# Graph attention and a routed feed-forward block on one core: seven loads move to SP's queue at batch 10, edge ends come in pairs, node features two blocks at a time

## The chip, the core and the metric

The kernel runs on one core of a Trainium2 chip. The core has a matrix engine (PE), a vector engine (DVE), an activation engine (ACT), GpSimd (POOL) and a synchronising engine (SP). Each has its own instruction stream; they meet only through semaphores. SP and ACT each issue transfers on a queue of their own (q1 and q10 in the profile), POOL issues gathers by index (q0). All transfers share 16 DMA engines. The metric is the device time of one execution in microseconds; lower is better.

## The reference

There are 12500 nodes with 256 features and 200000 edges sorted by target. A graph attention layer with 4 heads is followed by a feed-forward layer that is applied to the half of the nodes with the largest routing weight.

```python
src = jnp.concatenate([edge_index[0], loops])
dst = jnp.concatenate([edge_index[1], loops])
xp = (x @ W).reshape(n, H, C)
a_src = jnp.einsum('nhc,hc->nh', xp, att_src)
a_dst = jnp.einsum('nhc,hc->nh', xp, att_dst)
alpha = jax.nn.leaky_relu(a_src[src] + a_dst[dst], negative_slope=0.2)
ex = jnp.exp(alpha - amax[dst])
denom = jax.ops.segment_sum(ex, dst, num_segments=n)
w = ex / denom[dst]
msg = xp[src] * w[..., None]
agg = jax.ops.segment_sum(msg, dst, num_segments=n)
...
_, idx = jax.lax.top_k(weights, k)
sel = jnp.take_along_axis(x, sel_idx[:, :, None], axis=1)
h = jax.nn.gelu(jnp.einsum('bkd,dh->bkh', sel, w1) + b1)
y = jnp.einsum('bkh,hd->bkd', h, w2) + b2
...
x = x + gnn(layernorm(x), ...)
x = x + ffn(layernorm(x)[None], ...)[0]
```

## The kernel before

The nodes are cut into 98 blocks of 128. The program has three stages.

**The node stage** takes the blocks in 14 batches of 7 (`batches`). SP loads a batch of x into one of four rooms (`load_x`, L405; batch g+4 is loaded when batch g has been normalised). DVE takes statistics and normalises (`batch_stats`, `norm`, L1046), with POOL giving the reciprocal root (`rstd_batch`). PE transposes each block (L852), ACT copies the transposed block to SBUF (L710), PE multiplies it by the extended weight matrix (`project`, L829), ACT copies the product (`row_copy`, L698), and SP stores a finished batch to the table `node_rows` in HBM (`store_rows`, L417). The products have two rooms of a batch each, so ACT's first copy of batch g waits until the store of batch g-2 has landed. DVE's `keep_asd(g-2)` (L1050) waits for the last copy of batch g-2 and stands ahead of the statistics of batch g+1. In the last three batches DVE and PE also work out where each window's edges begin.

Before ACT makes its first copy it issues, one after the other on its own queue, two loads of edge targets (L677, L681) and seven loads of biases and weights (L682 to L689): b2, the attention bias, w1, w2, b1, the routing weights and the routing bias. b2 is split into parts by POOL after its last batch (`bias_parts`, L563 to L570); the other six are first waited for after the node stage.

**The window stage** has a window for each block of 128 targets (`two_by_two`, windows in pairs; b is 0 for even windows). POOL gathers 16 or 17 tiles of 128 source rows per window from `node_rows`, one indirect transfer per tile (L633), with the indices in `srci`. DVE makes one-hot matrices from the targets (L1202, L1206, L1212), looks up and forms the exponents (L1231 to L1239), and weighs the gathered rows (L1250); PE sums them by target (L948) and runs the feed-forward layer of earlier windows (L911, L926) between. In each window SP's order is: the targets of window w+1, broadcast as 16-bit numbers (`dbc`, L450), the same targets by partition (`dsti`, L434 and L436), then a wait until the gathers of window w-1 have landed, then the sources of window w+1 (`srci`, again L434 and L436), the features of block w (`base`, L487), and the block's own rows (`selfr`, L491). The two lines L434 and L436 are those of the helper `load_flat`; a transfer over 16 tiles and one over the last.

**The end** selects the half of the nodes by a search over the routing weights and adds their feed-forward rows.

Of the kernel before, what the change touches and what calls it, by code (L numbers as in the profile page):

```python
# [42 lines left out]
def build(nc, x, src, dst, W, att_src, att_dst, gbias, wr, br, w1, b1, w2, b2, out, N, E):  # L43
# [45 lines left out]
    with ExitStack() as ctx:  # L89
# [43 lines left out]
        srci = sb("srci", [P, 2, TILES], I32)  # L133
        dsti = sb("dsti", [P, 2, TILES], I32)
# [24 lines left out]
        xsrc = sb("xsrc", [P, 1], I32)  # L159
        xdst = sb("xdst", [P, 1], I32)  # L160
# [127 lines left out]
        def sems(names):  # L288
# [13 lines left out]
        ld_src, ld_dst, ld_dbc, ld_self, ld_x, gath, gath_last = (  # L302
            sem2(n) for n in ("ld_src", "ld_dst", "ld_dbc", "ld_self", "ld_x", "gath", "gath_last"))
# [11 lines left out]
        (x_src, x_dst, x_dbc, x_row, x_oht, x_step, x_oh, x_lk, x_dm, x_diff, x_ex, x_sc,  # L315
         x_go, x_done) = sems(
            "x_src x_dst x_dbc x_row x_oht x_step x_oh x_lk x_dm x_diff x_ex x_sc x_go x_done")

        m_src, m_dst, m_go, m_row, m_step, m_mask, m_tr, m_max, m_done = sems(
            "m_src m_dst m_go m_row m_step m_mask m_tr m_max m_done")  # L320
# [82 lines left out]
        def _(sp):  # L403
# [14 lines left out]

            def batch_io(g, t, b, r, q):
# [11 lines left out]
            def load_flat(into, edges, first, w, b, loaded):  # L431

                before = tiles_of(w) - 1
                sp.dma_start(into[:, b, 0:before], edges[bass.ds(first, before * P)].rearrange("(p t) -> p t", t=before)).then_inc(loaded, 16)  # L434
                with nc.allow_non_contiguous_dma("an edge to a partition"):
                    sp.dma_start(into[:, b, before:before + 1], edges[bass.ds(first + before * P, P)].rearrange("(p t) -> p t", t=1)).then_inc(loaded, 16)  # L436

# [4 lines left out]
            def load_sources(w, b, first):  # L442
                load_flat(srci, src, first, w, b, ld_src[b])

            def load_targets(w, b, first):
                if known(w, 2):

                    wait_apart(sp, (loc_ok, w - 1), (lk_ok, w - 1))
                flat = tiles_of(w) * P
                sp.dma_start(dbc[:, b, 0:flat], dst16_dram[bass.ds(first, flat)].rearrange("(a e) -> a e", a=1).broadcast_to([P, flat])).then_inc(ld_dbc[b], 16)  # L450
                load_flat(dsti, dst, first, w, b, ld_dst[b])

            load_sources(0, 0, first_edge(0))
# [15 lines left out]
            def exact_loads(w, j, k):  # L469
# [3 lines left out]
                with nc.allow_non_contiguous_dma("an edge to a partition"):  # L473
                    sp.dma_start(xsrc[:, :], src[bass.ds(first, P)].rearrange("(p t) -> p t", t=1)).then_inc(m_src, 16)
                    sp.dma_start(xdst[:, :], dst[bass.ds(first, P)].rearrange("(p t) -> p t", t=1)).then_inc(m_dst, 16)
# [19 lines left out]
            def extra_loads(w):  # L495
# [3 lines left out]
                def load(j, k):  # L499
# [4 lines left out]
                    with nc.allow_non_contiguous_dma("an edge to a partition"):  # L504
                        sp.dma_start(xsrc[:, :], src[bass.ds(at, P)].rearrange("(p t) -> p t", t=1)).then_inc(x_src, 16)
                        sp.dma_start(xdst[:, :], dst[bass.ds(at, P)].rearrange("(p t) -> p t", t=1)).then_inc(x_dst, 16)
# [37 lines left out]
        def _(pool):  # L544
# [60 lines left out]
            def gather_row(k, arrived, started):  # L605
# [4 lines left out]
                with pool.If(k < 1):  # L610
                    pool.sem_inc(started, 1)
                pool.indirect_dma_start(out=xrow[:, :], out_offset=None, in_=table,
                                        in_offset=bass.IndirectOffsetOnAxis(ap=xsrc[:, 0:1], axis=0)).then_inc(arrived, 16)

            def exact_gather(w, j, k):
                wait_apart(pool, (m_src, 16 * k + 16))
# [11 lines left out]
            def window(w, i, b):  # L628
                if not known(w, 2):
                    pool.wait_ge(ld_src[b], 32 * (i + 1))  # L630

                def gather(t, arrived):
                    pool.indirect_dma_start(out=rows[:, b, t, :], out_offset=None, in_=table,  # L633
                                            in_offset=bass.IndirectOffsetOnAxis(ap=srci[:, b, t:t + 1], axis=0)).then_inc(arrived, 16)

                last = tiles_of(w) - 1
                for t in range(last):
                    if known(w, 2) and t == 0:
                        wait_apart(pool, (ld_src[b], 32 * (i + 1)))
# [21 lines left out]
                def extra_gather(j, k):  # L661
                    wait_apart(pool, (x_src, 16 * k + 16))
# [8 lines left out]
        def _(act):  # L671
# [14 lines left out]
            with nc.allow_non_contiguous_dma("a bias by column of the hidden layer"):  # L686
                act.dma_start(b1s[:, :], b1.rearrange("(c p) -> p c", p=P)).then_inc(w_ld, 16)
            act.dma_start(wrs[:, :], bc(wr.rearrange("d o -> (d o)"), D)).then_inc(w_ld, 16)
# [774 lines left out]
```

## Time and profile before

| | |
|---|---|
| median of 3 runs | 2313.58 us (2313.06 to 2314.57) |
| the profiled execution | 2314.01 us, span of its trace 2312.2 us |
| busy: PE, DVE, POOL, ACT | 1896.5, 1609.1, 1594.0, 642.5 us |
| gathers (L633) | 1613, 1553.5 us busy |
| first gather begins, last gather begins | 149.19, 2193.30 us |
| mean granted PE clock | 0.894 of full speed |
| data moved | 365.43 MB in 244353 packets |

The span goes from the first to the last instruction of the trace. The node stage takes the first 149 us, the window stage goes on to about 2240 us, and the rest is selection and output. An engine's busy time leaves out the time in which it issues transfers, waits on semaphores or branches.

### The profile page before, as it was taken

The page shows a single profiled execution, that of the slowest core. Times are in us where ns is not written, and L with a number is a line of the kernel's source. Part 1 is how long each engine was busy: PE and PEld are TensorE (multiplying, and loading weights), DVE is VectorE, ACT ScalarE, POOL GpSimd, SP SyncE. Part 2 cuts the span into 40 slices and gives each one's busy share as a digit, 9 for nine tenths or more (in the row PEclk, how much of TensorE's full clock was granted, in tenths as well). Part 3 has the DMA queues.
Part 4 walks back from the last instruction along what each step waited for, and adds up shares of the span by engine and source line. Part 5 has one row for each costly group of instructions (what it writes and reads, how often), then busy time and mean ns, then how long its engine had stood idle before and what let it go on. Part 6 is the DMA issues. An engine that isn't in the chain of part 4 may idle for free.

```text
span 2312.2 us, 35972 instructions
## 1 busy us (share of the span) xinstructions
PE 1896.5 (82%) x9193; PEld 1610.2 (70%) x9194; DVE 1609.1 (70%) x3952; ACT 642.5 (28%) x1378; POOL 1594.0 (69%) x1675
## 2 busy tenths in 40 slices
PE   5955788888888888889888888888978888889871
PEld 4844677777777777777777777777767777777761
DVE  5756766766776667767767676777766677767748
ACT  3520222322332223322332233222322233222330
POOL 2257777777777777777777777777777777777700
PEclk9977899889899999989899999999989999999885
DMA  7645555555555555555555555555555555555448
GB/s 243 215 139 150 149 145 152 154 154 142 154 158 152 145 152 154 158 142 149 158 152 152 144 154 158 152 146 150 154 157 144 148 158 154 153 147 150 134 155 295
DMA packets 244353, 365.43 MB, mean 158 GB/s; under 512 B 90405, under 2 KB 179649, under 8 KB 244322
## 3 DMA queue, kind: packets, MB, share of 16 engines
q0 software_dynamic: 77488, 214.85, 35.0%
q1 hardware_dynamic: 150578, 134.33, 18.4%
q10 hardware_dynamic: 16256, 15.90, 2.0%
q8 instruction: 12, 0.20, 0.0%
q14 instruction: 19, 0.16, 0.0%
HBM read 326.04 MB, written 38.89 MB: 158 GB/s over the span
## 4 chain that ended last, share of the span: by engine, by line
POOL 34%; PE 25%; issue 23%; DVE 6%; POOLq 5%; DMA 4%; ACT 1%; ACTq 1%; DVEq 0%; SPq 0%
POOL rows L633 34%; PE ag_ps L948 13%; PE y_ps L926 4%; DMA rows<-node_rows,srci 3%; PE ag_ps L829 3%; POOLq L375 3%; PE h_ps L911 3%; DVE base L1438 2%; POOLq L652 1%; DVE rows L1250 1%; PE lk_ps L888 1%; PE tr_ps L852 0%; PE xl_ps L852 0%; DVE diff L1239 0%; ACT xl_ps L759 0%
## 5 line engine op out<-in xcount | busy, mean ns | idle before, releaser
L633 POOL DMA_INDIRECT rows<-node_rows,srci x1613 | 1553.5, 963 | 503.8 <-issue 474.5
L948 PE MATMUL ag_ps<-rows,oh 128*128 128x260 f32 x3322 | 921.6, 445 | 298.7 <-DVE rows L1250 297.8
L948 PEld LDWEIGHTS ag_ps<-rows,oh 128*128 128x128 f32 x3322 | 734.3, 225 | 456.0 <-issue 305.6
L1250 DVE TENSOR_TENSOR rows<-rows,xl_ps 128x768 f32<-128x768 f32 (+2 forms) x685 | 495.7, 793 | 36.4 <-ACT xl_ps L759 36.4
L926 PE MATMUL y_ps<-w2s,hT 128*128 128x256 f32 x1568 | 359.9, 383 | 6.9 <-ACT hT L740 6.9
L911 PE MATMUL h_ps<-xnT,w1s 128*128 128x256 f32 x1568 | 355.0, 379 | 0.0
L1231 DVE TENSOR_TENSOR zz<-rows,edge_dm 128x68 f32<-128x68 f32 x98 | 22.5, 229 | 470.5 <-DMA rows<-node_rows,srci 372.3
L926 PEld LDWEIGHTS y_ps<-w2s,hT 128*128 128x128 f32 x1568 | 300.7, 192 | 54.3 <-ACT hT L740 8.0
L759 ACT ACTIVATE xl_ps<-diff 128x68 f32<-128x68 f32 x98 | 22.6, 231 | 1110.2 <-DVE diff L1239 1099.7
L911 PEld LDWEIGHTS h_ps<-xnT,w1s 128*128 128x128 f32 x1568 | 297.6, 190 | 40.3
L1212 DVE TENSOR_TENSOR oh<-xl_ps,dloc 128x2176 f32<-128x2176 f32 x98 | 236.9, 2418 | 0.0
L740 ACT ACTIVATE hT<-h_ps,b1s 128x256 f32<-128x256 f32 x392 | 153.8, 475 | 1.2
L740 ACT ACT_TABLE_LOAD x98 | 125.7, 1283 | 49.4 <-ACT yb L749 34.3
L888 PE MATMUL lk_ps<-parts,dbc 128*128 (+1 forms) x1661 | 111.0, 206 | 20.0 <-DVE dbc L1202 20.0
L742 ACT ACT_TABLE_LOAD x98 | 125.7, 1283 | 1.8
L888 PEld LDWEIGHTS lk_ps<-parts,dbc 128*128 128x128 bf16 x1661 | 111.1, 160 | 20.9 <-issue 13.2
L829 PE MATMUL ag_ps<-hT,dbc 128*128 128x264 f32 x392 | 106.0, 394 | 13.4 <-ACT dbc L710 13.4
L793 ACT ACTIVATE steps_of_rows<-steps_of_rows 128x256 f32<-128x256 f32 x98 | 40.9, 417 | 199.9 <-DVE steps_of_rows L1294 199.9
L829 PEld LDWEIGHTS ag_ps<-hT,dbc 128*128 128x128 f32 x392 | 68.5, 195 | 20.9 <-issue 13.0
L1202 DVE TENSOR_SCALAR dbc<-dbc,node_id 128x2176 bf16<-128x2176 int16 x98 | 76.2, 777 | 0.0
L1219 DVE TENSOR_REDUCE edge_dm<-lk_ps 128x136 f32<-128x408 f32 x98 | 56.4, 576 | 16.1 <-issue 16.0
L588 POOL TENSOR_SCALAR rs_b<-selfr 128x7 f32<-128x7 f32 x14 | 3.9, 279 | 87.4 <-DVE selfr L1060 79.3
(183 smaller groups left out, 1322.0 us busy)
## 6 DMA issues: line engine op xcount, KB each, us to landing
dbc<-dst SPq DMA_DIRECT2D x97, 544.0 KB
rows<-node_rows,srci POOLq DMA_INDIRECT x1613, 2.7
selfr<-node_rows SPq DMA_DIRECT2D x98, 130.0 KB, 3.0
base<-in_x SPq DMA_DIRECT2D x14, 896.0 KB, 5.2
base<-in_x SPq DMA_DIRECT2D x98, 128.0 KB, 2.3
ffn_rows<-yb ACTq DMA_DIRECT2D x48, 256.0 KB, 3.3
node_rows<-base SPq DMA_DIRECT2D x13, 910.0 KB, 5.7
out<-base SPq DMA_DIRECT2D x3, 1024.0 KB, 5.8
```

The costliest lines, as they stand in the source:

```text
L375: return eng.value_load(win[0:1, bass.ds(COLS * w + k, 1)], min_val=0, max_val=most)
L633: pool.indirect_dma_start(out=rows[:, b, t, :], out_offset=None, in_=table, in_offset=bass.IndirectOffsetOnAxis(ap=srci[:, b, t:t + 1], ax ...
L740: last = nc.scalar.activation(hT[:, m, :], h_ps[:, m * PAIR:(m + 1) * PAIR], ACT.Gelu_apprx_tanh, bias=b1s[:, n:n + 1])
L742: nc.scalar.preload_act_table_set(EXP_AND_LN)
L829: last = nc.tensor.matmul(ag_ps[parity % 2][:, 0:WIDE], xnT2[:, parity % 2, c, :], wext[:, c, :], start=(c == 0), stop=(c == DC - 1))
L888: last = nc.tensor.matmul(lk_ps[:, VK * t:VK * (t + 1)], by_tile[:, t, :] if t < before else oht[:, b, before * P:(before + 1) * P], node_ ...
L911: last = nc.tensor.matmul(h_ps[:, m * PAIR:(m + 1) * PAIR], w1s[:, c, n * P:(n + 1) * P], xnT[:, c, :], start=(c == 0), stop=(c == DC - 1))
L926: last = nc.tensor.matmul(y_ps[:, a * D:(a + 1) * D], hT[:, m, a * P:(a + 1) * P], w2s[:, half * HALF + m, :], start=False, stop=(half == ...
L948: product = nc.tensor.matmul(ag_ps[b][:, 0:ROW], oh[:, b, t, :], rows[:, b, t, :], start=(t == 0), stop=False)
L1202: nc.vector.tensor_scalar(oht[:, b, 0:flat], dbc[:, b, 0:flat], node_id[:, bass.ds(w, 1)], None, ALU.is_equal).then_inc(oht_ok, 1)
L1212: nc.vector.tensor_tensor(oh[:, b, 0:n, :], iota_ps.unsqueeze(1).broadcast_to([P, n, P]), dloc[:, 0:n].unsqueeze(2).broadcast_to([P, n, P] ...
L1250: nc.vector.tensor_tensor(v, v, e, ALU.mult).then_inc(scaled[k], 1)
```

## The change

Three things are changed, and nothing of what is computed.

1. The seven loads of L682 to L689 leave ACT's stream. They are issued by SP in the same order (`load_weights`), in the turn of batch 10, right after the store of batch 9.
2. The host hands over sources and targets as one array of pairs, `edges`. `srci` and `dsti` become one tile `ends` with the two numbers side by side. Its two transfers are issued where those of the sources were, behind the wait for the gathers of window w-1. The gathers read their index from `ends[:, b, t, 0:1]`, and L1206 reads its targets from `ends[:, b, 0:n, 1]`, each with a step of 8 bytes between tiles where it was 4. For window 0 both ends are loaded at the start of the program, where only the sources were.
3. The features are loaded for two blocks at once, in the even windows.

```diff
+            def load_weights():
+
+                sp.dma_start(bias_f[0], bc(b2, D)).then_inc(b2_ld, 16)
+                sp.dma_start(gbs[:, :], bc(gbias, D)).then_inc(w_ld, 16)
+                sp.dma_start(w1s[:, :, :], w1.rearrange("(c p) n -> p c n", p=P)).then_inc(w_ld, 16)
+                sp.dma_start(w2s[:, :, :], w2.rearrange("(c p) n -> p c n", p=P)).then_inc(w_ld, 16)
...
@@ batch_io
                 if known(g, 1):
                     store_rows(g - 1, 1 - b)
+                if isinstance(g, int) and g == NB - DEEP:
+                    load_weights()
...
+            def load_ends(w, i, b, first):
+                if known(w, 2):
+
+                    wait_apart(sp, (gath[b], 16 * (TILES - 1) * i), (gath_last[b], 16 * i), (loc_ok, w - 1))
                 before = tiles_of(w) - 1
-                sp.dma_start(into[:, b, 0:before], edges[bass.ds(first, before * P)].rearrange("(p t) -> p t", t=before)).then_inc(loaded, 16)
+                sp.dma_start(ends[:, b, 0:before, :], edges[bass.ds(first, before * P), :].rearrange("(p t) v -> p t v", t=before)).then_inc(ld_ends[b], 16)
                 with nc.allow_non_contiguous_dma("an edge to a partition"):
-                    sp.dma_start(into[:, b, before:before + 1], edges[bass.ds(first + before * P, P)].rearrange("(p t) -> p t", t=1)).then_inc(loaded, 16)
+                    sp.dma_start(ends[:, b, before:before + 1, :], edges[bass.ds(first + before * P, P), :].rearrange("(p t) v -> p t v", t=1)).then_inc(ld_ends[b], 16)
...
@@ SP, window
                     load_targets(w + 1, 1 - b, first)
-                    if known(w, 1):
-
-                        wait_apart(sp, (gath[1 - b], 16 * (TILES - 1) * (i + b)), (gath_last[1 - b], 16 * (i + b)))
-                    load_sources(w + 1, 1 - b, first)
-                sp.dma_start(base[:, bass.ds(w, 1), :].rearrange("p w c -> p (w c)"), x[bass.ds(w * P, P), :]).then_inc(ld_x[b], 16)
+                    load_ends(w + 1, i + b, 1 - b, first)
+                if b == 0:
+                    sp.dma_start(base[:, bass.ds(w, 2), :], nodes(x, w, 2)).then_inc(ld_x, 16)
...
@@ POOL, window
-                                            in_offset=bass.IndirectOffsetOnAxis(ap=srci[:, b, t:t + 1], axis=0)).then_inc(arrived, 16)
+                                            in_offset=bass.IndirectOffsetOnAxis(ap=ends[:, b, t, 0:1], axis=0)).then_inc(arrived, 16)
...
@@ ACT
-            act.dma_start(bias_f[0], bc(b2, D)).then_inc(b2_ld, 16)
-            act.dma_start(gbs[:, :], bc(gbias, D)).then_inc(w_ld, 16)
-            act.dma_start(w1s[:, :, :], w1.rearrange("(c p) n -> p c n", p=P)).then_inc(w_ld, 16)
-            act.dma_start(w2s[:, :, :], w2.rearrange("(c p) n -> p c n", p=P)).then_inc(w_ld, 16)
...
@@ DVE, one_hots_turned
-                nc.vector.tensor_scalar(dloc[:, 0:n], dsti[:, b, 0:n], base_id[:, bass.ds(w, 1)], None, ALU.subtract).then_inc(loc_ok, 1)
+                nc.vector.tensor_scalar(dloc[:, 0:n], ends[:, b, 0:n, 1], base_id[:, bass.ds(w, 1)], None, ALU.subtract).then_inc(loc_ok, 1)
```

Line numbers of the changed kernel differ by a few. ACT's stream before, at its beginning: the loads of edge targets (`oh`), of b2 (`rows`), gbs, w1s, w2s, b1s, wrs and brs, and then the first copies of transposed blocks.

```order
L677 DMA oh<-in_dst 128x1600
L681 DMA oh<-in_dst 127x1
L682 DMA rows<-in_L_ffn_b 128x256
L683 DMA gbs<-in_L_gnn_bias 128x256
L684 DMA w1s<-in_L_ffn_w 128x2x1024
L685 DMA w2s<-in_L_ffn_w 128x8x256
L687 DMA b1s<-in_L_ffn_b 128x8x1
L688 DMA wrs<-in_L_ffn_wr 128x256
L689 DMA brs<-in_L_ffn_br 128x1
L710 COPY dbc<-tr_ps 128x256
L710 COPY dbc<-xl_ps 128x256
L698 COPY base<-ag_ps 128x264
```

The same place now:

```order
L682 DMA oh<-in_dst 128x1600
L686 DMA oh<-in_dst 127x1
L707 COPY dbc<-tr_ps 128x256
L707 COPY dbc<-xl_ps 128x256
L695 COPY base<-ag_ps 128x264
L707 COPY dbc<-tr_ps 128x256
```

The first copy now follows the two loads of targets directly. SP's stream before, from the last four whole stores of the node stage (batches 9 to 12) to the last piece of batch 13:

```order
L417 DMA node_rows<-base 128x7x260 x4
L450 DMA dbc<-dst 128x2176
L434 DMA dsti<-in_dst 128x16
L436 DMA dsti<-in_dst 128x1
L458 DMA window_table<-wi 98x6
L417 DMA node_rows<-base 128x5x260
L461 DMA win<-window_table 1x588
L417 DMA node_rows<-base 128x2x260
```

The same place now:

```order
L415 DMA node_rows<-base 128x7x260
L419 DMA rows<-in_L_ffn_b 128x256
L420 DMA gbs<-in_L_gnn_bias 128x256
L421 DMA w1s<-in_L_ffn_w 128x2x1024
L422 DMA w2s<-in_L_ffn_w 128x8x256
L424 DMA b1s<-in_L_ffn_b 128x8x1
L425 DMA wrs<-in_L_ffn_wr 128x256
L426 DMA brs<-in_L_ffn_br 128x1
L415 DMA node_rows<-base 128x7x260 x3
L460 DMA dbc<-dst 128x2176
L467 DMA window_table<-wi 98x6
L415 DMA node_rows<-base 128x5x260
```

The seven loads stand between the stores of batches 9 and 10, and the two small loads of targets ahead of the window table are gone. SP's stream in an odd window before (the rows without a transfer are register work and waits):

```order
L450 REGISTER_ALU
L450 DMA dbc<-dst 128x2176
L434 REGISTER_ALU
L434 DMA dsti<-in_dst 128x16
L436 ISA
L436 DMA dsti<-in_dst 128x1
L369 ISA
L434 DMA srci<-in_src 128x16
L436 DMA srci<-in_src 128x1
L487 ISA
L487 DMA base<-in_x 128x256
L491 ISA
```

The same place now:

```order
L460 REGISTER_ALU
L460 DMA dbc<-dst 128x2176
L367 ISA
L451 REGISTER_ALU
L451 DMA ends<-in_edges 128x32
L453 ISA
L453 DMA ends<-in_edges 128x2
L497 ISA
L497 DMA selfr<-node_rows 128x260
```

Both ends of the edges now stand behind the wait (the ISA row ahead of them), two transfers are gone from each window, and a third from each odd one.

## Rows read from the trace of the kernel before

**Rows 1.** The page: busy time of the engines, share of the span, instructions

```profile
PE 1896.5 (82%) x9193; PEld 1610.2 (70%) x9194; DVE 1609.1 (70%) x3952; ACT 642.5 (28%) x1378; POOL 1594.0 (69%) x1675
```

**Rows 2.** Line L633: duration ns min/median/max; idle before it until, us, times

```profile
L633 POOL DMA_INDIRECT rows<-node_rows,srci x1613: 942/947/1572, 149.2 to 2193.3; - x180
...
  issue: 474.5, 1556
  DMA node_rows<-base: 12.2, 1
  PE lk_ps L888: 9.4, 31
  PE ag_ps L948: 7.6, 25
```

**Rows 3.** Timeline of POOL, first and last gather: start, duration, [idle before]

```profile
149.19 1.12 POOL L633 DMA_INDIRECT rows<-node_rows,srci  x1 [12.22 <-DMA node_rows<-base]
...
2193.30 0.95 POOL L633 DMA_INDIRECT rows<-node_rows,srci  x1 [0.30 <-issue]
```

**Rows 4.** Timeline of ACT, 9 to 26 us (ACTq: its issuing of transfers)

```profile
9.60 0.52 ACTq L681 DMA_DIRECT2D oh<-in_dst  x1
10.15 6.13 ACTq L682 DMA_DIRECT2D rows<-in_L_ffn_b  x1
16.31 0.44 ACTq L683 DMA_DIRECT2D gbs<-in_L_gnn_bias  x1
...
17.79 3.38 ACTq L687 DMA_DIRECT2D b1s<-in_L_ffn_b  x1
21.19 3.92 ACTq L688 DMA_DIRECT2D wrs<-in_L_ffn_wr  x1
...
25.64 0.37 ACT L710 COPY dbc<-tr_ps 128x256 f32<-128x256 f32 x1 [23.28 <-issue]
```

**Rows 5.** Timeline of PE, first blocks and block 14

```profile
12.48 0.66 PE L852 MATMUL tr_ps<-ident,rows 128*128 128x128 f32 x2 [9.95 <-DVE rows L1046]
...
26.16 2.10 PE L829 MATMUL ag_ps<-hT,dbc 128*128 128x264 f32 x4 [12.59 <-ACT dbc L710]
...
44.37 0.38 PE L852 MATMUL tr_ps<-ident,rows 128*128 128x128 f32 x2
```

**Rows 6.** Timeline of DVE, batches 1 and 2

```profile
20.49 3.96 DVE L1046 TENSOR_SCALAR rows<-base,selfr,rs_b 128x256 f32<-128x256 f32 x7
38.22 0.21 DVE L1050 COPY oh<-base 128x56 f32 x1 [13.77 <-ACT base L698]
...
41.33 2.32 DVE L1046 TENSOR_SCALAR rows<-base,selfr,rs_b 128x256 f32<-128x256 f32 x7
```

**Rows 7.** Timeline of SP's queue, stores of batches 9, 10, 11 and after

```profile
109.18 0.38 SPq L417 DMA_DIRECT2D node_rows<-base  x1
118.67 0.38 SPq L417 DMA_DIRECT2D node_rows<-base  x1
129.42 0.38 SPq L417 DMA_DIRECT2D node_rows<-base  x1
...
139.38 0.88 SPq L436 DMA_DIRECT2D dsti<-in_dst  x1
140.42 0.40 SPq L458 DMA_DIRECT2D window_table<-wi  x1
...
145.69 0.24 SPq L461 DMA_DIRECT2D win<-window_table  x1
146.04 0.40 SPq L417 DMA_DIRECT2D node_rows<-base  x1
```

**Rows 8.** Stretches: length, PE, PEld, DVE, ACT, POOL busy (count), PEclk, DMA share, GB/s

```profile
115.00:120.00 5.00, 3.51 (x19) 2.72 (x18) 3.75 (x18) 2.06 (x6) 1.97 (x2) 1.00 0.09 32
```

**Rows 9.** Transfers of the run: KB each, median us from issue to landing

```profile
node_rows<-base SPq DMA_DIRECT2D x13, 910.0 KB, 5.7
...
srci<-in_src SPq DMA_DIRECT2D x98, 0.5 KB, 2.2
```

**Rows 10.** Timeline of ACT, the last copy of the node stage

```profile
144.45 0.38 ACT L698 COPY base<-ag_ps 128x264 f32<-128x264 f32 x1 [0.51 <-PE ag_ps L829]
```

**Rows 11.** Timeline of SP's queue and DVE, a window of the middle

```profile
1015.20 0.33 SPq L434 DMA_DIRECT2D srci<-in_src  x1
...
1030.92 0.23 DVE L1206 TENSOR_SCALAR dloc<-dsti,base_id 128x17 f32<-128x17 int32 x1
```

More of the change, by code:

```diff
@@ L40, in sizes, with build @@
     return nw, tiles, ep
-def build(nc, x, src, dst, W, att_src, att_dst, gbias, wr, br, w1, b1, w2, b2, out, N, E):
+def build(nc, x, edges, dst, W, att_src, att_dst, gbias, wr, br, w1, b1, w2, b2, out, N, E):
     D = W.shape[0]
@@ L132, in build @@
         rows = sb("rows", [P, 2, TILES, ROW])
-        srci = sb("srci", [P, 2, TILES], I32)
-        dsti = sb("dsti", [P, 2, TILES], I32)
+        ends = sb("ends", [P, 2, TILES, 2], I32)
         dbc = sb("dbc", [P, 2, FLAT], I16)
@@ L157, in build @@
         wcol = sb("wcol", [P, 2])
[L159 to L160 removed]
+        xends = sb("xends", [P, 2], I32)
         xdbc = sb("xdbc", [P, P], I16)
@@ L300, in build @@
             "count_ok before_ok win_ok gmax_ok gall_ok exact_ok sdiff_ok exself_ok parts_ok pre")
-        ld_src, ld_dst, ld_dbc, ld_self, ld_x, gath, gath_last = (
-            sem2(n) for n in ("ld_src", "ld_dst", "ld_dbc", "ld_self", "ld_x", "gath", "gath_last"))
+        ld_ends, ld_dbc, ld_self, gath, gath_last = (sem2(n) for n in ("ld_ends", "ld_dbc", "ld_self", "gath", "gath_last"))
+        ld_x = sem("ld_x")
         y_st = sem("y_st")
@@ L417, in store_rows @@
                 sp.dma_start(nodes(table, g * BATCH + at, count), po[b][:, at:at + count, 0:ROW]).then_inc(tab_st[b], 16)
+            def load_weights():
[3 more added lines that the diff above has]
+                sp.dma_start(w2s[:, :, :], w2.rearrange("(c p) n -> p c n", p=P)).then_inc(w_ld, 16)
+                with nc.allow_non_contiguous_dma("a bias by column of the hidden layer"):
+                    sp.dma_start(b1s[:, :], b1.rearrange("(c p) -> p c", p=P)).then_inc(w_ld, 16)
+                sp.dma_start(wrs[:, :], bc(wr.rearrange("d o -> (d o)"), D)).then_inc(w_ld, 16)
+                sp.dma_start(brs[:, :], bc(br, 1)).then_inc(w_ld, 16)
             def batch_io(g, t, b, r, q):
@@ L429, in batch_io @@
                     sp.dma_start(dst16_dram.rearrange("(p e) -> p e", p=P), dst16).then_inc(d16_st, 16)
[L431 to L436 removed]
             def first_edge(w):
                 return 0 if isinstance(w, int) and w == 0 else entry(sp, w, 0, EP - FLAT)
[L442 to L443 removed]
+            def load_ends(w, i, b, first):
+                if known(w, 2):
+                    wait_apart(sp, (gath[b], 16 * (TILES - 1) * i), (gath_last[b], 16 * i), (loc_ok, w - 1))
+                before = tiles_of(w) - 1
+                sp.dma_start(ends[:, b, 0:before, :], edges[bass.ds(first, before * P), :].rearrange("(p t) v -> p t v", t=before)).then_inc(ld_ends[b], 16)
+                with nc.allow_non_contiguous_dma("an edge to a partition"):
+                    sp.dma_start(ends[:, b, before:before + 1, :], edges[bass.ds(first + before * P, P), :].rearrange("(p t) v -> p t v", t=1)).then_inc(ld_ends[b], 16)
             def load_targets(w, b, first):
                 if known(w, 2):
[L448 removed]
+                    wait_apart(sp, (lk_ok, w - 1))
                 flat = tiles_of(w) * P
                 sp.dma_start(dbc[:, b, 0:flat], dst16_dram[bass.ds(first, flat)].rearrange("(a e) -> a e", a=1).broadcast_to([P, flat])).then_inc(ld_dbc[b], 16)
[L451 to L453 removed]
+            load_ends(0, 0, 0, first_edge(0))
             batches(sp, batch_io, last_peeled=True)
@@ L473, in exact_loads @@
                 with nc.allow_non_contiguous_dma("an edge to a partition"):
-                    sp.dma_start(xsrc[:, :], src[bass.ds(first, P)].rearrange("(p t) -> p t", t=1)).then_inc(m_src, 16)
-                    sp.dma_start(xdst[:, :], dst[bass.ds(first, P)].rearrange("(p t) -> p t", t=1)).then_inc(m_dst, 16)
+                    sp.dma_start(xends[:, :], edges[bass.ds(first, P), :]).then_inc(m_ends, 16)
             if_exact(sp, exact_loads)
```

43 lines of the change are left out of this document (19 added, 24 removed).

## The prediction

> **What bounds the kernel now.** I read the page first. PE is busy 82% of the span and POOL 69% [rows 1], which points at PE. The question for a change to transfers, though, is who waits for whom, so I went on to the gathers. The instruction of one gather has a median of 947 ns, and there are 1613; the idle time ahead of them is 474.5 us in 1556 pieces that end with "issue" [rows 2], which is 0.30 us each: it is what POOL needs between two gathers, not a wait. The 56 pieces laid to PE make 9.4 + 7.6 = 17.0 us [rows 2], again 0.30 each. So POOL waits for nobody from its first gather at 149.19 to the end of its last at 2193.30 + 0.95 = 2194.25 [rows 3]. These 2045.06 us are POOL's own pace, 1.27 us for each gather. PE's higher share is work that fits beside it.
>
> Two things follow. Whatever makes transfers of the window stage cheaper changes nothing unless it changes a gather's own 0.95 + 0.30 us. And whatever lets the first gather begin earlier moves all that follows by as much. The one real wait of the gathers is 12.2 us for the table [rows 2], at the end of the node stage.
>
> Next I followed the node stage back. PE has transposed the first block at 12.48 + 0.66 = 13.14, and then stands idle until 26.16, for 12.59 us, released by ACT's copy L710 [rows 5]. ACT starts that copy at 25.64 [rows 4]. What it did before is issuing: from 10.15 to 25.60 seven loads leave its queue. Three of them hold it for 6.13, 3.38 and 3.92 us, the other four, of which one row stands, for 0.44 to 0.49 us [rows 4]. These loads are needed only 100 us later. From 26 us on, block follows block on PE.
>
> **What the change costs and gives, part by part.**
>
> *ACT's seven loads go.* ACT is then free at 9.60 + 0.52 = 10.12 [rows 4], and the copy waits for the transposed block at 13.14 [rows 5]. So it starts at 13.14 instead of 25.64: 12.50 us earlier. I checked what is late next. DVE's normalising of batch 1 ends at 20.49 + 3.96 = 24.45, and its next step, L1050, stood at 38.22 after 13.77 us of waiting for ACT's copies [rows 6]; shifted by 12.5 it would start at 25.7, still after 24.45. Batch 2 is normalised from 41.33 and its first block transposed at 44.37 [rows 5, 6], so even a DVE that is late has 3.0 us before PE feels it. The first load of block rows has less company, since 2.4 MB of weights are out of its way. I take the whole 12.5.
>
> A rule speaks against so large a number. By these rows an issue can hold an engine for 6.13 us [rows 4]. The Trainium skill (DMA: Bandwidth & Descriptors, section on issuing engines that are not separate DMA queues) says that issuing from several engines saves only the sequencer's own time, which is usually small beside the transfer. By that rule the gain would be only what seven undisturbed issues take, rival 2 below. The trace disagrees with "usually small" here: 13.4 of 15.5 us are three long issues.
>
> *SP's seven loads come.* Undisturbed they take 7 x 0.44 = 3.1 us; as on ACT, at the time when the DMA engines were full, 15.5 us [rows 4]. They follow the store of batch 9 at 109.18; the next store is due at 118.67, 9.49 us later [rows 7]. By the lower bound nothing is late. By the upper, the store of batch 10 goes out at 109.56 + 15.5 = 125.1 and has landed 5.7 us later [rows 9], at 130.8. Who waits is ACT's first copy of batch 12, which comes a block's time after the store of batch 11 at 129.42 [rows 7]. A block takes (144.45 - 26.16) / 97 = 1.22 us [rows 5, 10], which gives 130.6: 0.2 us late. The stretch is emptier than the start, 0.09 of the DMA engines' time near 118 us [rows 8], so I go nearer to the lower bound and take 0. POOL's split of b2 comes after its last batch, three batches on, and the other six are needed after 149 us.
>
> *The last steps before the first gather.* The window table leaves at 140.42, and the wait for its landing holds SP until 145.69; the last store goes at 146.04 [rows 7]. Ahead of the table on the queue stood the two loads of targets (the second at 139.38 [rows 7]), now gone. The table may land sooner, but the last store also needs ACT's last copy, 144.45 + 0.38 = 144.83 [rows 10]. The gain lies between 0 and 145.69 - 144.83 = 0.9; I take 0.4.
>
> *Both ends in one transfer, two blocks at once.* In two windows SP issues 14 transfers before and 9 now. In the window stage SP mostly waits for gathers to land, so its issue time is covered, and POOL does not wait for its indices: they are issued at 1015.20 [rows 11], and a window of POOL is 17 x 1.27 = 21.6 us long. New is that the targets are behind that wait too. They are needed by L1206 at 1030.92, and small loads land 2.2 us after issue [rows 9], at about 1018: 13 us to spare. If that cover were gone, DVE would be late in one-hots and not in gathers, up to some microseconds of PE's slack. The features are wanted a window after they are issued. Cost and gain 0.
>
> *A gather's own time.* Its index is read with a step of 8 bytes. No row shows such a gather. From below: an instruction cannot gain from it that I can see, 0, though what lies over the median is 1553.5 - 1613 x 0.947 = 26 us, which a shift of DVE's work against the gathers could alter. From above: nothing excludes a few ns. One index per partition is read either way, and median and minimum are 5 ns apart over all tiles and both buffers [rows 2], so its place does not matter now. I take 0.
>
> **The sum.** 2312.2 - 12.5 - 0.4 = 2299.3 us of span. The profiled execution took 2314.01 us, which becomes 2301.1. It is 0.4 above the median of 2313.58, so the median becomes 2300.7.
>
> **The rivals.** A measurement of this kernel can tell about 0.2%, 4.6 us, from no change.
>
> 1. *The seven loads hold SP, and the node stage gives part back.* SP would be late with the store of batch 10 by more than my bound, because the stores themselves fill the queue. For: stores of 910 KB are on the same queue. Against: the idle DMA engines of rows 8. With 1 to 6 us given back: 2301.7 to 2306.7.
> 2. *Only the plain issue time is saved,* 3.1 us, because something else than ACT's issuing holds the first blocks, a load of features or DVE. Time 2310.5 (this is also what the page's rule gives). Against: PE's transposed block waits from 13.14 on [rows 5]. A milder form, in which DVE or a load of x takes over part, gives a gain of 6 to 10 us: 2303.6 to 2307.6.
> 3. *Gathers become slower through the step of 8 bytes.* This is the rival of the other sign. It eats the gain at 12.9 / 1613 = 8 ns per gather. At 2% of 947 ns, 19 ns, it costs 30.6 us: 2331.3. Against: the narrow spread in rows 2.
> 4. *Gathers become faster,* since DVE's work meets them at another moment or fewer small packets are about. At a third to two thirds of the 26 us above the median: 2283 to 2292; a few us of it is more likely than all.
>
> **How the numbers follow.** My forecast, 2297 to 2304, has 0.70. Rival 1 has 0.07, the milder form of rival 2 0.07, its full form 0.03, rival 3 0.04, rival 4 0.07, and 0.02 are left for a fall to no change at all. The likeliest gives the time, 2300.7. The range takes in rival 1 and most of the milder rival 2 above, and small forms of rival 4 below: 2294 to 2307. It leaves out some 0.16. Faster by over 0.2% means below 2309.0: 0.70 + 0.07 + 0.07 + 0.07 = 0.91. Within 0.2%: 0.03 + 0.02 = 0.05, and slower 0.04.
>
> **What would show it.** ACT's first copy near 13.1 us and no idle 12.59 us on PE. L1050 of batch 0 near 25.7. The seven loads on SP's queue between 97 and about 104 us, and the store of batch 10 near 106. The window table's landing a little shorter than 5.3 us. The first gather at 149.19 - 12.9 = 136.3 and the last at about 2180.4, with 1613 gathers of median 947 ns and 0.30 us between. L1206 without idle time before it. I am wrong if the gathers' stage is not 2045 us long, or if the first gather comes later than 140.

## The result and the profile after

The changed kernel takes 2300.48 us (median of 5 runs, 2298.90 to 2302.37), the kernel before 2313.06 in the same comparison (5 runs). The ratio is 0.9946, with a 95% interval of 0.9931 to 0.9960: 12.6 us faster. A second comparison on a chip of the same pace, further down as after_third, gave 2298.27 against 2312.26, ratio 0.9940 (0.9926 to 0.9953). The forecast was 2300.7 in 2294 to 2307.

The profiled execution took 2298.9 us, with a span of 2297.1. First the page's busy times; nothing in them tells where the time went, since PE only does the same work in a shorter span [rows 1].

```profile
PE 1889.9 (82%) x9193; PEld 1605.7 (70%) x9194; DVE 1608.6 (70%) x3952; ACT 642.4 (28%) x1378; POOL 1594.2 (69%) x1675
```

The gathers (line L638 now), as in [rows 2]: duration in ns, first and last start, and the idle time ahead of them.

```profile
L638 POOL DMA_INDIRECT rows<-node_rows,ends x1613: 942/946/1565, 137.4 to 2180.8; - x180
...
  issue: 473.8, 1555
  DMA node_rows<-base: 12.8, 1
  PE lk_ps L885: 11.0, 36
  PE ag_ps L945: 6.4, 21
```

POOL's timeline at the first and the last gather, as in [rows 3]:

```profile
137.44 1.11 POOL L638 DMA_INDIRECT rows<-node_rows,ends  x1 [12.81 <-DMA node_rows<-base]
...
2180.79 0.94 POOL L638 DMA_INDIRECT rows<-node_rows,ends  x1 [0.30 <-issue]
```

The gathers are the same gathers, at the same pace, and begin 11.75 us earlier. The three stages, cut at the first gather and at the end of the last (columns as in [rows 8]), of before:

```profile
0.00:149.19 149.19, 117.38 (x607) 95.83 (x608) 96.91 (x370) 68.05 (x200) 40.46 (x63) 1.00 0.65 207
149.19:2194.25 2045.06, 1724.56 (x8351) 1468.55 (x8352) 1437.08 (x3292) 548.94 (x1135) 1553.52 (x1613) 0.90 0.54 151
2194.25:2312.00 117.75, 54.61 (x237) 45.78 (x235) 75.12 (x292) 25.51 (x43) 0.00 (x0) 0.74 0.67 222
```

and of after:

```profile
0.00:137.44 137.44, 115.74 (x607) 94.40 (x608) 97.59 (x371) 67.90 (x200) 41.14 (x63) 0.99 0.72 225
137.44:2181.74 2044.30, 1722.19 (x8358) 1467.74 (x8359) 1435.92 (x3291) 549.00 (x1135) 1553.11 (x1613) 0.90 0.53 151
2181.74:2297.00 115.26, 51.92 (x229) 43.55 (x227) 75.14 (x292) 25.52 (x43) 0.00 (x0) 0.75 0.69 227
```

The span fell by 11.75 + 0.76 + 2.6 = 15.1 us. The last 2.6 us are the stage behind the last gather (117.95 and 115.36 us to the end of the span), and I count them as no gain: after_again and after_third, which are the same changed kernel, take 118.2 and 119.1 us for it, and the other ten traces of the experiments 117.1 to 119.2.

ACT at the start, against [rows 4]: the loads of targets, and then at once the copy.

```profile
8.69 0.40 ACTq L682 DMA_DIRECT2D oh<-in_dst  x1
9.14 0.53 ACTq L686 DMA_DIRECT2D oh<-in_dst  x1
13.57 0.37 ACT L707 COPY dbc<-tr_ps 128x256 f32<-128x256 f32 x1 [11.22 <-PE tr_ps L849]
```

What it waits for is now named: PE's transpose, which ended at 12.88 + 0.66 = 13.54, and no longer "issue". PE, against [rows 5], with the last projection of the node stage:

```profile
12.88 0.66 PE L849 MATMUL tr_ps<-ident,rows 128*128 128x128 f32 x2 [10.35 <-DVE rows L1043]
...
14.09 2.10 PE L826 MATMUL ag_ps<-hT,dbc 128*128 128x264 f32 x4
...
22.97 0.44 PE L849 MATMUL xl_ps<-ident,rows 128*128 128x128 f32 x2 [1.12 <-DVE rows L1043]
...
130.14 1.95 PE L826 MATMUL ag_ps<-hT,dbc 128*128 128x264 f32 x8
```

The first projection begins 26.16 - 14.09 = 12.07 us earlier. The last stood in the trace of before at

```profile
142.47 1.95 PE L829 MATMUL ag_ps<-hT,dbc 128*128 128x264 f32 x8
```

so it begins 12.33 us earlier: the lead is kept over all 98 blocks. There is one new wait on the way, 1.12 us for DVE, which normalises batch 1 (`norm`) while PE takes batch 0:

```profile
20.89 3.97 DVE L1043 TENSOR_SCALAR rows<-base,selfr,rs_b 128x256 f32<-128x256 f32 x7
24.88 0.21 DVE L1047 COPY oh<-base 128x56 f32 x1
```

L1047 (L1050 in [rows 6]) starts at 24.88, where the prediction had 25.7, and has no idle time before it any more, where it had 13.77 us. It now waits for DVE's own normalising and not for ACT.

SP's queue from the store of batch 9 on, against [rows 7]:

```profile
96.85 0.38 SPq L415 DMA_DIRECT2D node_rows<-base  x1
97.28 0.56 SPq L419 DMA_DIRECT2D rows<-in_L_ffn_b  x1
...
100.50 1.65 SPq L424 DMA_DIRECT2D b1s<-in_L_ffn_b  x1
102.19 4.80 SPq L425 DMA_DIRECT2D wrs<-in_L_ffn_wr  x1
107.03 0.43 SPq L426 DMA_DIRECT2D brs<-in_L_ffn_br  x1
107.59 0.40 SPq L415 DMA_DIRECT2D node_rows<-base  x1
```

The seven hold SP for 107.46 - 97.28 = 10.2 us, and the store of batch 10 goes at 107.59 where 118.67 - 12.5 = 106.2 was due. Nobody was late for it: PE's only wait of over 0.5 us between 96 and 127 us is one of 1.49 for DVE, which before had as well. The last steps on SP:

```profile
128.09 0.41 SPq L467 DMA_DIRECT2D window_table<-wi  x1
130.58 0.41 SPq L415 DMA_DIRECT2D node_rows<-base  x1
133.93 0.24 SPq L470 DMA_DIRECT2D win<-window_table  x1
134.27 0.39 SPq L415 DMA_DIRECT2D node_rows<-base  x1
```

SP is released from the window table's landing 133.93 - 128.09 = 5.84 us after its issue, against 145.69 - 140.42 = 5.27 before, although the two small loads are gone from ahead of it.

### The profile page after: what moved, and what is told of

The parts are those of the page before. It is cut to its first block, busy times and chain, and to the rows that moved or that the text cites. A ratio compares the mean times of both kernels' runs of the same rounds, so it can differ in the third digit from the quotient of the medians.

```text
span 2297.1 us, 35535 instructions
## 1 busy us (share of the span) xinstructions
PE 1889.9 (82%) x9193; PEld 1605.7 (70%) x9194; DVE 1608.6 (70%) x3952; ACT 642.4 (28%) x1378; POOL 1594.2 (69%) x1675
## 3 DMA queue, kind: packets, MB, share of 16 engines
q1 hardware_dynamic: 124498, 136.80, 18.8%
## 4 chain that ended last, share of the span: by engine, by line
POOL 34%; PE 27%; issue 22%; DVE 6%; POOLq 5%; DMA 5%; ACT 1%; DVEq 0%; ACTq 0%; SPq 0%
POOL rows L638 34%; PE ag_ps L945 15%; DMA rows<-node_rows,ends 4%; PE y_ps L923 4%; PE h_ps L908 3%; POOLq L373 3%; PE ag_ps L826 2%; DVE base L1435 2%; POOLq L657 1%; DVE rows L1247 1%; PE lk_ps L885 1%; DVE selfr L1053 1%; DMA node_rows<-base 1%; DVE diff L1236 0%; DVE zz L1228 0%
## 5 line engine op out<-in xcount | busy, mean ns | idle before, releaser
L638 POOL DMA_INDIRECT rows<-node_rows,ends x1613 | 1553.1, 963 | 504.0 <-issue 473.8
L885 PEld LDWEIGHTS lk_ps<-parts,dbc 128*128 128x128 bf16 x1661 | 111.0, 160 | 21.0 <-issue 12.9
L793 ACT ACTIVATE lnv<-vareps 128x1 f32<-128x1 f32 x98 | 19.9, 203 | 153.5 <-DVE vareps L1303 153.5
```

Source lines behind the costliest of these rows:

```text
L885: last = nc.tensor.matmul(lk_ps[:, VK * t:VK * (t + 1)], by_tile[:, t, :] if t < before else oht[:, b, before * P:(before + 1) * P], node_ ...
```

## The experiments

Twelve experiments ran, four on each of three chips; two of them (after_again, after_third) are the changed kernel once more. The kernel before takes 2721.0 us on the chip of the first four (34 runs) and 2748.8 on that of the next four (34 runs), against 2312 to 2313 where the result and the last four runs were made. The node stage keeps its times there, but POOL, whose gathers have a median of 946 to 949 ns, pauses more between them, and single runs of one kernel lie up to 35 us apart. So I read from these eight runs the node stage by its rows, and from the medians only the sign: a gain or cost of some 5 us is not to be told from none there. The table gives for each the start of ACT's first copy, of PE's last projection and of the first gather, in us.

| run | ACT's first copy | last projection | first gather | ratio to before (95%) |
|---|---|---|---|---|
| before | 25.64 | 142.47 | 149.19 | |
| changed kernel | 13.57 | 130.14 | 137.44 | 0.9946 (0.9931 to 0.9960) |
| w_only | 14.14 | 130.85 | 138.28 | 0.9939 (0.9921 to 0.9957) |
| ends_only | 26.08 | 142.49 | 149.65 | 0.9996 (0.9977 to 1.0015) |
| pair_only | 25.41 | 141.69 | 148.68 | 1.0005 (0.9984 to 1.0026) |
| after_again | 13.71 | 130.47 | 137.56 | 0.9958 (0.9939 to 0.9977) |
| act_batch10 | 13.28 | 137.74 | 144.75 | 0.9963 (0.9934 to 0.9991) |
| sp_start | 13.78 | 132.83 | 139.75 | 0.9942 (0.9912 to 0.9971) |
| three_long | 20.57 | 136.80 | 143.76 | 0.9960 (0.9936 to 0.9984) |
| two_big | 19.21 | 136.21 | 142.87 | 0.9976 (0.9951 to 1.0000) |
| after_third | 13.36 | 129.68 | 136.82 | 0.9940 (0.9926 to 0.9953) |
| targets_late | 13.71 | 130.21 | 136.51 | 0.9945 (0.9931 to 0.9958) |
| store_first | 14.07 | 129.60 | 136.23 | 0.9950 (0.9936 to 0.9963) |
| both_late | 13.31 | 129.94 | 135.91 | 0.9944 (0.9930 to 0.9957) |

**The three parts, each alone.** w_only is the kernel before with only the seven loads moved:

```diff
                 if known(g, 1):
                     store_rows(g - 1, 1 - b)
+                if isinstance(g, int) and g == NB - DEEP:
+                    load_weights()
...
-            act.dma_start(bias_f[0], bc(b2, D)).then_inc(b2_ld, 16)
-            act.dma_start(gbs[:, :], bc(gbias, D)).then_inc(w_ld, 16)
...
```

> The kernel before with the seven loads moved to SP at batch 10 and nothing else. My theory (ACT's issuing held the first blocks): ACT's first copy near 13.2 us instead of 25.6, the first gather 11.5 to 12.5 us earlier than 149.2, a median 12 to 13 us below the kernel before. Rival (the gain is shared with the joined loads, or needs them): 8 us or less. Rival (the short fall of the node stage, 11.75 instead of 12.9 us, comes from the joined loads): then the first gather is 12.9 us earlier here.

ends_only joins only the two ends of the edges (`ends` for `srci` and `dsti`, behind the wait for the gathers):

```diff
-                    load_sources(w + 1, 1 - b, first)
+                    load_ends(w + 1, i + b, 1 - b, first)
```

> The kernel before with both ends of an edge in one transfer and nothing else: indices with a step of 8 bytes, targets behind the wait for the gathers, no loads of targets ahead of the window table. My theory: gathers with a median of 946 to 947 ns, a window stage within 1 us of 2045.1, the first gather within 0.5 us of 149.2, a median within 2 us of the kernel before. Rival (slower gathers): over 8 ns more per gather, 13 us or more slower. Rival (fewer small packets help): 2 us or more faster, with a shorter window stage.

pair_only loads only the features for two blocks at once:

```diff
-                sp.dma_start(base[:, bass.ds(w, 1), :].rearrange("p w c -> p (w c)"), x[bass.ds(w * P, P), :]).then_inc(ld_x[b], 16)
+                if b == 0:
+                    sp.dma_start(base[:, bass.ds(w, 2), :], nodes(x, w, 2)).then_inc(ld_x, 16)
```

> The kernel before with the features loaded for two blocks at once and nothing else. My theory: hidden behind SP's wait for gathers, a median within 1.5 us of the kernel before and a window stage within 1 us of 2045.1. Rival (a transfer of 256 KB in the way of the block's own rows or of the gathers): 2 us or more slower, with later landings of selfr.

after_again is the changed kernel, unaltered.

> The changed kernel once more, beside the parts on one chip. If the parts add up: a median 12 to 13 us below the kernel before, within 1.5 us of the seven loads alone. The profile shows once more how long the stretch after the last gather is (117.95 us before, 115.36 us in the first profile of the change): if the change shortens it, it is near 115.4 here and in the parts that carry the cause, and near 118 in the others; if it varies by itself, it varies without order.

w_only has the gain: first gather at 138.28, ratio 0.9939. That gather is 10.9 us earlier than before, a little less than the 11.5 to 12.5 expected; but from ACT's first copy to the last projection it takes 116.71 us, as the changed kernel does (116.57 and, in after_again, 116.76), so nothing of the node stage's gain is missing. Its median is 17.4 us below the kernel before and that of after_again 14.8, where 12 to 13 were expected, and the two are 2.6 us apart, where 1.5 were: the scatter of this chip covers both. The other two begin their gathers at 149.65 and 148.68, as before, and their ratios don't differ from 1 (intervals of 0.2% to either side). The step of 8 bytes in a gather's index costs nothing: median 946 ns in ends_only and in w_only, which reads with a step of 4.

**Is it the engine that issues, or the time at which it does?** act_batch10 is the changed kernel with the seven loads back on ACT, but in its turn of batch 10 (ACT's last four batches are written out for it, where they were part of its loop):

```diff
             def batch_copies(g, turn, b, r, q):
+                if isinstance(g, int) and g == NB - DEEP:
+                    act.dma_start(bias_f[0], bc(b2, D)).then_inc(b2_ld, 16)
...
+                    act.dma_start(brs[:, :], bc(br, 1)).then_inc(w_ld, 16)
```

> The changed kernel with the seven loads given back to ACT, but in its turn of batch 10 and not at the start. My theory (what costs is that ACT is held at a moment when PE waits for it): the loads hold ACT for 3 to 10 us between two copies of the node stage, PE waits about as long, and the first gather is later than in the changed kernel by that much less what DVE's slack absorbs: 2 to 9 us. Rival (the cost was the company of the loads at the start): no later than the changed kernel.

Its ACT timeline:

```profile
97.15 5.12 ACTq L692 DMA_DIRECT2D wrs<-in_L_ffn_wr  x1
102.30 0.46 ACTq L693 DMA_DIRECT2D brs<-in_L_ffn_br  x1
102.85 0.37 ACT L703 COPY dbc<-tr_ps 128x256 f32<-128x256 f32 x1 [7.98 <-issue]
```

and its PE timeline behind that:

```profile
103.27 2.13 PE L822 MATMUL ag_ps<-hT,dbc 128*128 128x264 f32 x4 [6.64 <-ACT dbc L703]
...
105.62 1.97 PE L822 MATMUL ag_ps<-hT,dbc 128*128 128x264 f32 x4
```

The stretch of these blocks, with columns as in [rows 8]:

```profile
103.00:108.00 5.00, 4.73 (x13) 3.70 (x14) 4.43 (x6) 1.90 (x6) 0.00 (x0) 0.50 0.98 270
```

A load of 128 KB in an issue of 5.12 us, at 97 us in the program, stops ACT just as at the start. PE waits 6.64 us, and then takes 2.13 and 1.97 us for what takes it 1.06 elsewhere: in this stretch the granted clock is 0.50, the lower of its two levels (1.2 of 2.4 GHz). The first gather comes at 144.75, 7.2 us later than in after_again. At both places that were tried a long issue on ACT is in PE's way; on SP 10.2 us of issuing at batch 10 are in nobody's way.

sp_start has the seven loads on SP, but at the program's start, behind the first load of ends:

```diff
             load_ends(0, 0, 0, first_edge(0))
+            load_weights()
             batches(sp, batch_io, last_peeled=True)
```

> The changed kernel with the seven loads on SP at the very start, behind the edge ends of window 0. The DMA engines carry the same bytes at the start as in the kernel before, only ACT is not held. My theory: ACT's first copy near 13.6 us, first gather within 1.5 us of the changed kernel's 137.4, the same median within 2 us. Rival (the 2.4 MB in the way of the first batches was the cost): first copies or batches 2 to 5 wait for features, and 5 us or more of the gain are lost.

The two longest of its issues on SP, in the timeline:

```profile
15.50 3.59 SPq L424 DMA_DIRECT2D b1s<-in_L_ffn_b  x1
19.13 3.91 SPq L425 DMA_DIRECT2D wrs<-in_L_ffn_wr  x1
```

The DMA engines are as full as they were before (share of 1.10 in 20 to 25 us, 1.06 before, 0.08 in the changed kernel), and the first copy still comes at 13.78. The last projection is 132.83 against 130.47 in after_again: 2.4 us of the 12 come from the loads' absence at that time, and the rest from ACT's freedom alone. The first gather comes 2.2 us later than in after_again, more than the 1.5 of my theory and less than the 5 of the rival. Where the 2.4 us arise stands in ACT's timeline, at the cast of the edge targets, first in sp_start and then in the changed kernel:

```profile
24.65 1.52 ACT L699 CAST dbc<-oh 128x1600 int16<-128x1600 int32 x1 [2.00 <-DMA oh<-in_dst]
```

```profile
22.16 1.53 ACT L700 CAST dbc<-oh 128x1600 int16<-128x1600 int32 x1
```

With the weights on the same DMA engines the targets land 2 us after ACT wants them. PE waits 2.94 us for ACT behind that, and its granted clock averages 0.71 in 25 to 30 us, between its two levels (1.2 and 2.4 GHz), where it is 1.00 in the changed kernel.

**Which issue is long?** three_long moves only b2, b1 and the routing weights, whose issues held ACT for 6.13, 3.38 and 3.92 us [rows 4]; the other four stay on ACT:

```diff
+            act.dma_start(gbs[:, :], bc(gbias, D)).then_inc(w_ld, 16)
+            act.dma_start(w1s[:, :, :], w1.rearrange("(c p) n -> p c n", p=P)).then_inc(w_ld, 16)
+            act.dma_start(w2s[:, :, :], w2.rearrange("(c p) n -> p c n", p=P)).then_inc(w_ld, 16)
+            act.dma_start(brs[:, :], bc(br, 1)).then_inc(w_ld, 16)
+
             def row_copy(n, g, t, b, turn):
```

> The changed kernel, but only the three loads that held ACT long (b2, b1, routing weights) are issued by SP at batch 10; the four short ones (attention bias, w1, w2, routing bias) stay on ACT at the start. If a long issue belongs to the load itself: ACT is held for 4 x 0.45 = 1.8 us, its first copy is near 13.6 us and the whole gain stays. If it belongs to a full queue: some of the four become long, and the first copy is later than 14.5 us.

Its ACT timeline:

```profile
9.82 6.09 ACTq L683 DMA_DIRECT2D gbs<-in_L_gnn_bias  x1
15.94 0.45 ACTq L684 DMA_DIRECT2D w1s<-in_L_ffn_w  x1
16.41 0.84 ACTq L685 DMA_DIRECT2D w2s<-in_L_ffn_w  x1
17.28 3.25 ACTq L686 DMA_DIRECT2D brs<-in_L_ffn_br  x1
20.57 0.37 ACT L707 COPY dbc<-tr_ps 128x256 f32<-128x256 f32 x1 [18.21 <-issue]
```

The load of gbs took 0.44 in second place and takes 6.09 in first; that of brs, 128 numbers, takes 3.25. The long issue goes with the place, not with the load. two_big moves only w1 and w2, 1 MB each, and leaves five small loads on ACT.

```diff
+            act.dma_start(bias_f[0], bc(b2, D)).then_inc(b2_ld, 16)
+            act.dma_start(gbs[:, :], bc(gbias, D)).then_inc(w_ld, 16)
...
+            act.dma_start(wrs[:, :], bc(wr.rearrange("d o -> (d o)"), D)).then_inc(w_ld, 16)
+            act.dma_start(brs[:, :], bc(br, 1)).then_inc(w_ld, 16)
```

> The changed kernel, but only the two loads of 1 MB (w1, w2) are issued by SP at batch 10; the five small ones stay on ACT at the start. If the queue's fill makes the long issues: b2's 6 us stays (it stood ahead of the big ones), b1 and the routing weights are short, ACT's first copy comes near 18.5 us and the first gather 5 us later than in the changed kernel. If b1 and the routing weights are long by themselves (many small pieces): the first copy is near 25 us.

```profile
10.59 6.14 ACTq L681 DMA_DIRECT2D rows<-in_L_ffn_b  x1
...
17.23 0.46 ACTq L684 DMA_DIRECT2D b1s<-in_L_ffn_b  x1
17.72 0.85 ACTq L685 DMA_DIRECT2D wrs<-in_L_ffn_wr  x1
```

Without the 2 MB ahead of them, b1 and the routing weights take 0.46 and 0.85 instead of 3.38 and 3.92. The first load behind the two of targets takes 6.1 us whatever it is. So the later long issues come from w1 and w2 ahead of them. SP's issues at batch 10 agree: b1 and the routing weights take 1.65 and 4.80 us in the changed kernel, behind w1 and w2, and 1.14 and 1.11 in three_long without them. By its place the first long issue would come from the 800 KB of targets or from the 127 single numbers loaded right behind them (L681 before), but no run took either away, so its cause stays open. The Trainium skill (DMA: Bandwidth & Descriptors, section on issuing engines that are not separate DMA queues) says that issuing from several engines saves only the sequencer's time to start a transfer, usually small beside the transfer. These runs show up to 6.14 us for one issue, so here that time was not small.

**The last steps before the first gather.** The term for the window table had come out with the wrong sign, so the last four runs went there. after_third is the changed kernel.

> The changed kernel, unaltered, as the control beside the next three. If its times of the node stage repeat: first copy of ACT near 13.5 us, last projection near 130.3, window table issued near 128.3 and SP released from its landing 5.2 to 5.8 us later, last store near 134, first gather near 137.5. On a chip like the last two the median is not 2300 but 2700 to 2750 us, with a ratio of 0.994 to 0.997 to the kernel before.

targets_late issues window 0's broadcast of targets (`dbc`, L460) behind the last store instead of ahead of the window table:

```diff
-            sp.wait_ge(d16_st, 16)
-            load_targets(0, 0, first_edge(0))
...
             store_rows(NB - 1, 1, BATCH - EDGE, EDGE)
+            sp.wait_ge(d16_st, 16)
+            load_targets(0, 0, first_edge(0))
```

> The changed kernel, but the broadcast load of window 0's targets (dbc, L460) is issued behind the last store instead of ahead of the window table. It was issued at 125.70 us, 2.4 us ahead of the window table, and spreads 4 KB to 128 partitions. Theory A: the window table's landing of 5.2 to 5.8 us is long because this load stands ahead of it on SP's queue. Then SP is released after about 4 us, the last store goes when ACT's last copy has ended (132.5), and the first gather comes at about 136, 1 to 1.7 us before the control's. Theory B: the landing is the path to HBM and back, and who is ahead does not matter: landing and first gather as in the control, within 0.4 us. Either way the window stage keeps its length, and the median moves by at most 0.1%, which it can hardly tell.

store_first issues the last store ahead of the wait for the window table and its load back (`win`):

```diff
+            store_rows(NB - 1, 1, BATCH - EDGE, EDGE)
             sp.wait_ge(win_st, 16)
...
-            store_rows(NB - 1, 1, BATCH - EDGE, EDGE)
```

> The changed kernel, but SP issues the last store of rows (two blocks) before it waits for the window table's landing, not behind it. Theory A: the last store goes out as soon as ACT's last copy has ended, at about 132.6 us instead of 134.0 to 134.3, and the first gather comes 1.4 to 1.7 us earlier, near 136.0. The window table's return load then goes out at about 134, as before. Theory B: the first gather also waits for something that the return load feeds (the window's first register values), or the two transfers meet: then no gain, 137.5. The median moves by 0.1% at most.

both_late has both edits.

> The changed kernel with both edits: the last store ahead of the wait for the window table, and the load of window 0's targets behind it. If the last store alone decides when the first gather begins, it gives what the store alone gives, about 136.0, and the load's place adds nothing; if the load's place ahead of the last store matters too (its packets are ahead of the store's), the first gather comes up to 0.5 us earlier still. The median moves by 0.1% at most.

SP's queue in after_third:

```profile
127.64 0.41 SPq L467 DMA_DIRECT2D window_table<-wi  x1
130.12 0.41 SPq L415 DMA_DIRECT2D node_rows<-base  x1
133.35 0.24 SPq L470 DMA_DIRECT2D win<-window_table  x1
133.69 0.39 SPq L415 DMA_DIRECT2D node_rows<-base  x1
```

and in targets_late:

```profile
128.16 0.41 SPq L465 DMA_DIRECT2D window_table<-wi  x1
130.65 0.41 SPq L415 DMA_DIRECT2D node_rows<-base  x1
131.49 0.25 SPq L468 DMA_DIRECT2D win<-window_table  x1
132.64 0.38 SPq L415 DMA_DIRECT2D node_rows<-base  x1
```

The wait for the table falls from 133.35 - 127.64 = 5.71 to 131.49 - 128.16 = 3.33 us: it is the broadcast of 544 KB ahead of it that makes it long. SP's last store now waits for ACT's last copy, which ended at 132.57. This is one trace for each kernel, but the other two fit: in both_late, without the broadcast ahead, SP is past the wait 4.9 us after the issue at the latest (132.81 - 127.90, and it had the last store to issue before that), and in store_first, with the broadcast ahead, 5.27 us after it (132.82 - 127.55).

The gain at the first gather is smaller than that: against after_third it comes 0.31 us earlier in targets_late, 0.59 in store_first and 0.91 in both_late, where 1 to 1.7 were expected of either edit. Since the whole program shifts by some tenths from run to run, I take the time from the start of the last projection to the first gather: 7.14 in after_third, 6.30 in targets_late, 6.63 in store_first, 5.97 in both_late. The ten other traces lie between 6.66 and 7.43. So both_late is 1.2 us quicker than after_third, targets_late 0.8, and store_first, with 0.5, hardly outside the scatter. Each of these is one trace, and after_third stands near the upper end of the scatter (7.14), so the gains may be smaller still. The last store, issued at 133.69, 132.64, 132.03 and 132.38 in these four, takes 2.24, 2.97, 3.31 and 2.65 us to its landing in the chain that ended last. The three that go earlier take 0.4 to 1.1 us longer. Part of the gain is given back, I suppose because the store of five blocks, issued 2.0 us ahead of it in these three and 3.6 us in after_third, is then still being written; no run tests that. The medians, 2298.27, 2299.21, 2299.77 and 2298.95 us with spreads of 3 to 5 us each, can't tell a gain of 1.2 us. A kernel that is measurably faster than the changed one was not found.

## Why the prediction was right

**ACT's seven loads: -12.5 us.** Right in mechanism and nearly in size. The copy began at 13.57 and not at 13.14, since the program's start was itself 0.4 us later in this execution (13.36 and 14.07 in others). The first projection gained 12.07 us and the last 12.33. w_only shows that this part alone gives the gain of the node stage. What I had not split: 2.4 us of it are the company of the loads, which makes ACT wait for the edge targets, and not ACT's issuing (sp_start).

**What is late next.** Here the working had a gap. I checked DVE's L1050 and PE's need of batch 2, and not PE's need of batch 1, which is normalised to 24.86 while PE is free from about 22: a wait of 1.12 us. A second one is on ACT, 2.01 us for the landing of the first store, with 0.96 us on PE; before, PE lost 0.84 at another place. They cost nothing in the end: from the first to the last projection PE takes 116.05 us, before 116.31.

**SP's seven loads: 0.** Right. They took 10.2 us, between the bounds of 3.1 and 15.5 but not near the lower one where I had put them ("between 97 and about 104": to 107.5). The stretch of [rows 8] looked empty, but the stores and the loads fill it themselves: the DMA share is 0.80 and 1.10 in 100 to 110 us. The store of batch 10 was 1.4 us late against the 106.2 that was due, and nobody waited, so rival 1 did not come.

**The window table: -0.4.** This step failed. I had put the landing down to the two small loads of targets ahead of it. It took 5.84 us instead of 5.27, and lies between 5.0 and 5.8 in all eleven traces that keep the broadcast ahead and the store behind the wait: 5.3, 5.5 and 5.6 in the three with the two small loads, 5.0 to 5.8 in the eight without. targets_late shows the cause: the broadcast, which I had not counted because the change left it where it was. The distance from last projection to first gather came out at 7.30 against 6.72, +0.6 instead of -0.4, within its scatter.

**Both ends in one transfer, two blocks at once, the gather's own time: 0 each.** Nothing speaks against it, but the medians could not show less than some 5 us (ends_only 0.9996, pair_only 1.0005, each with 0.0019 to 0.0021 to either side). L1203, which reads the targets, has no idle time ahead of it in any of its 98 instances. The window stage took 2043.8 to 2044.6 us in the five traces of kernels with the change on chips of this pace, against 2045.06 in the one of before: some 0.5 to 1.2 us less. Whether this is the change or that one execution stays open. Rivals 3 and 4 fall: 946 against 947 ns, and what lies above the median is 1553.1 - 1613 x 0.946 = 27 us, as before.

**Rival 2,** by which only 3.1 us are saved, falls with ACT's first copy, 12.07 us earlier, and so does its milder form.

**The sum** gave 2300.7, and the median is 2300.48. In the trace the first gather gained 11.75 us and not 12.9, and the window stage gave 0.76 that was not in the sum. The kernel before also came out at 2313.06, half a microsecond below the 2313.58 that I had reckoned from. So the gain was 12.6 us and not 12.9, and the agreement to 0.2 us is partly luck.

## What to carry to other kernels

Look in the timeline of a computing engine for its transfer issues before its first work: a row of several us on a queue is that engine standing still, and idle time with "issue" behind it is where this shows. Move such loads to an engine that computes nothing and to a time at which they are not needed yet; moving them in time alone, on the same engine, moved the stall (144.75 against 137.56). Ahead of a short transfer that somebody waits for, look at everything that the same engine has issued shortly before, above all at broadcasts, not only at what the change touches.

## What was not expected of the hardware

- Which load holds the queue depends on its place: one of 128 numbers held ACT for 3.25 us, and the same load 0.43 to 0.60 us elsewhere.
- After a pause of 6.64 us PE came back at a granted clock of 0.50 and took twice as long for two blocks; with that, a stall of 8 us on ACT at batch 10 came out as 7.2 us at the first gather.
- A broadcast of 544 KB, issued 2.4 us ahead of a table of 98 x 6 numbers, lengthened the wait for that table's landing by 2.4 us (5.71 against 3.33, one trace of each).
- The same kernel takes 2312 to 2313 us where the result and the last four runs were made, and 2721 and 2749 on the chips of the other eight, with gathers of nearly the same median (946 to 949 ns). The difference lies in the window stage, 2447 to 2488 us there. POOL's pauses that end with "issue" grew from 474 us to 591 to 641; 175 to 200 us more end with "remote" (a semaphore from elsewhere by the profile), and 91 to 115 us are laid to PE (L888 before) where it was 9. The mean granted clock is 0.842 to 0.850 against 0.894. So "POOL waits for nobody" holds on the chips of the result and of the last four runs, and not on those two. What causes the difference was not looked into.
